# Eight layer steps on one core: VectorE takes q and k ahead of its norm steps in attention 0, the first stacks are loaded by head halves, the last layer's roots move from GpSimd to ScalarE, and two blocks end without GpSimd's drain

## The chip, the cores and the metric

One Trainium2 chip, one core of it. The metric is the device time of one launch in microseconds. The kernel before took 2697.12 us, the median of three runs (2694.36, 2697.12 and 2703.2).

## The reference, cut to what matters

Four layers, each an attention step and a feed-forward step, on 16 batches of 256 tokens by 128 channels (4096 tokens). Every attention has 16 heads. Each of the eight steps is x = _layernorm(x + step(x)), with this normalisation of each token:

```python
def _layernorm(x, axis=-1, eps=1e-05):
    m = jnp.mean(x, axis=axis, keepdims=True)
    v = jnp.var(x, axis=axis, keepdims=True)
    return (x - m) / jnp.sqrt(v + eps)
```

Attention 0 has heads of 64 channels, so that its q, k and v have 1024 columns; attentions 1 to 3 have heads of 8. Attention 1 takes the softmax of negated distances, attention 3 is causal:

```python
# attention 0
Q = (x @ Wq.T + bq).reshape(B, N, H, HD)
K = (x @ Wk.T + bk).reshape(B, N, H, HD)
V = (x @ Wv.T + bv).reshape(B, N, H, HD)
scores = jnp.einsum('bnhd,bmhd->bhnm', Q, K)
w = jax.nn.softmax(scores * (SCALE * adaptive_scale)[None, :, None, None] / TEMP, axis=-1)
attn = jnp.einsum('bhnm,bmhd->bnhd', w, V).reshape(B, N, H * HD)
y = x + (attn @ Wo.T + bo)
mu, var = jnp.mean(y, axis=-1, keepdims=True), jnp.var(y, axis=-1, keepdims=True)
return (y - mu) / jnp.sqrt(var + EPS) * gamma + beta      # then x = _layernorm(x + this)
```

So attention 0 has two normalisations, an inner one with gamma and beta and the outer one of the step. Feed-forward 3, the last step, sends each token to two of eight experts with limited places, adds both weighted results to those of a shared expert, and ends with a normalisation, which is the program's output. The inverse roots of that last normalisation are the ones that the change moves.

## The kernel before

Each of the eight steps is one block of the program: attn0 (`attention_wide`), ffn0 (`routed_layer`), attn1 (`attention_dist`), ffn1, attn2 (`attention_small`), ffn2 (`sign_mlp`), attn3 (`attention_small`, causal) and ffn3 (`routed_layer` with two places for each token, `cap2`). The tokens stand in SBUF as `x_state`, 32 tiles of 128 tokens by 128 channels. The five engines run from one order each, written out by hand by loops over slots, and meet by semaphores. A block ends with each engine's drain and a barrier, then its semaphores are cleared on GpSimd and there is a second barrier (L2785 and L2786).

**Attention 0** (L51 to L484). A unit is two heads of one batch; a batch has U = 8 units, and a slot is one unit. Z_AT, A_AT + 1 and W_AT say in which slot of a batch the steps of the two normalisations run on VectorE: `inner_norm` (L437), `outer_stats` (L419 and L422) and `write_x` (L448). They are even slots. VectorE also takes the maxima of the scores (`row_max`, L399), adds the bias to q and k of the unit two slots ahead (`take_qk`, L410, which empties the PSUM bank `A_M`), turns sums around (`invert`, L404), and in odd slots copies a transposed tile (`take_turned`, L415). `A_M` is one bank shared by the projections of q and k (L255), of v (L263), the transposes of x (L245) and the output projection (L307); before each of them TensorE waits in `bank_free` until the last user's result has been taken. The affine part of the norm, `A_s` (L205 and L208), is GpSimd's; so are the normalised probabilities (L185). ScalarE has the exponentials (L355), the copies of v (`A_V`, L348) and others.

**Attentions 1 to 3.** The projected q and k of a batch are cut into three bf16 parts, stored to DRAM (L621; L1217 in attention 1) and read back stacked on partitions: `stack(b)` on SP's queue issues three loads of `A_QS` and three of `A_KS`, each 24 rows of 16 heads x 256 columns. TensorE's `score(n)` waits for all six of its batch at the first head. In attention 1 the first head also waits for the squared lengths (`n2_in`), whose DMAs stand behind the stack on the same queue.

**Feed-forward 3, its end.** GpSimd fetches with indirect DMAs (`fetch`, L1892) each token tile's result from the second of its experts, 32 fetches in eight groups of four. For each group g VectorE does `add_first` (L2449 and L2453), `add_second` (L2460), `norm_stats` (L2467, L2470 and L2472, which gives `L_veps`) and `write` (L2477, `L_shift`). The root of each group is one GpSimd instruction, `tensor_tensor` with `pow` and an exponent of -0.5 (L1919), put between the fetches of later groups. ScalarE writes the normalised tiles (L2190), after it has copied eight groups of transposed coefficients from PSUM (`L_coefT`, L2186); those come from TensorE's `turn_coef(g)` (L2048), which alternates with the products with them (L2059). A product waits until VectorE has taken the result two groups before. SP stores `out` in eight pieces (L1873).

## Time and profile before

| | |
|---|---|
| profiled execution | 2692.44 us, span 2690.7 us, mean granted clock 0.911 of full speed |
| median of three runs | 2697.12 us |
| busy share of the span | PE 84%, PEld 60%, DVE 59%, ACT 58%, POOL 51% |
| attn0, 0 to 684 us; the rest of the slices below is ffn0 to ffn3 | PE 95.7 to 97.1% busy in each of five stretches of 100 us between 100 and 600 us |
| last block, ffn3 | 2407.7 to 2690.7 us |

The page shows the span in 40 slices of 67 us, each digit the busy share in tenths:

```profile
PE   5999999998294899998399958999799699976783
DVE  3566666666412899998623327667454466643465
ACT  3666666665152899998145524667544277651352
POOL 2454554555235888863133155654321488735346
PEclk9999999999596799999599969999899799987995
```

The time of an execution is the span and a little around it (1.7 us in this one). Small groups of waits matter here, not the shares: the program is a row of eight stages with different limits.

### The profile page before, as it was taken

The numbers are of one execution on the slowest core, as the hardware profiler recorded it, in microseconds if no ns is written. First come the engines' busy times: TensorE is split into PE (matmuls) and PEld (weight loads), VectorE is DVE, ScalarE is ACT, GpSimd is POOL, SyncE is SP. The second block draws the span as 40 slices with busy tenths as digits, with TensorE's granted clock in tenths as the row PEclk, the third lists the DMA queues.
The fourth block names the chain that finished last, engine by engine and source line by source line (L and its number), as shares of the span: only waits on it lengthen the run. The fifth ranks groups of instructions, "written<-read, shape, count | busy, mean of one in ns | idle before, by whom it ended". The sixth has DMA issues, their size and how long they took to land. (4 is left out here: it accounts for less than half of the span.)

```text
span 2690.7 us, 52551 instructions
## 1 busy us (share of the span) xinstructions
PE 2248.2 (84%) x17832; PEld 1619.0 (60%) x17832; DVE 1593.5 (59%) x4357; ACT 1572.2 (58%) x3828; POOL 1361.9 (51%) x2164
## 2 busy tenths in 40 slices
PE   5999999998294899998399958999799699976783
PEld 3667667666193566665289934555345477754682
DVE  3566666666412899998623327667454466643465
ACT  3666666665152899998145524667544277651352
POOL 2454554555235888863133155654321488735346
PEclk9999999999596799999599969999899799987995
DMA  4000000000312322210311134332000333311232
GB/s 164 1 1 1 2 1 1 1 1 1 119 56 69 99 63 80 71 59 1 134 44 47 38 82 115 92 100 80 2 1 1 87 108 100 98 40 52 74 120 74
DMA packets 106506, 153.46 MB, mean 57 GB/s; under 512 B 17330, under 2 KB 78660, under 8 KB 99204
## 3 DMA queue, kind: packets, MB, share of 16 engines
q1 hardware_dynamic: 93956, 127.24, 15.3%
q0 software_dynamic: 12288, 22.86, 3.4%
q8 instruction: 148, 2.42, 0.4%
q14 instruction: 114, 0.93, 0.1%
HBM read 100.87 MB, written 47.19 MB: 55 GB/s over the span
## 5 line engine op out<-in xcount | busy, mean ns | idle before, releaser
L185 POOL TENSOR_SCALAR A_prob<-A_prob,A_rinv 128x256 f32<-128x256 f32 x512 | 254.3, 514 | 325.4 <-DVE A_rinv L404 325.4
L1011 DVE TENSOR_REDUCE A_nmax<-A_S 128x2 f32<-128x512 f32 (+1 forms) x512 | 311.5, 621 | 173.6 <-PE A_S L788 83.5
L940 ACT ACTIVATE A_PT<-A_E 128x512 f32<-128x512 f32 (+1 forms) x512 | 273.0, 551 | 142.3 <-PE A_E L811 65.8
L355 ACT ACTIVATE A_prob<-A_S,A_nmax 128x256 f32<-128x256 f32 x512 | 236.7, 488 | 102.9 <-DVE A_nmax L399 102.9
L1885 POOL DMA_INDIRECT L_xe<-rows,L_index x112 | 106.5, 950 | 231.3 <-PE L_k L1976 112.2
L1608 DVE TENSOR_SCALAR_CACHE_REDUCE A_D<-A_S 128x256 f32<-128x256 f32 x512 | 193.5, 417 | 14.8 <-PE A_S L1391 14.4
L1614 DVE COPY A_PT<-A_T 128x512 f32<-128x512 f32 x256 | 175.3, 687 | 19.4 <-PE A_T L1404 19.3
L1404 PE MATMUL A_T<-ident_sb,A_D 128*128 128x128 f32 x1024 | 160.5, 280 | 27.9 <-ACT A_D L1533 15.1
L2031 PE MATMUL L_k<-L_w,L_hT 128*128 (+1 forms) x1216 | 171.3, 279 | 12.3 <-ACT L_hT L2177 10.7
L2031 PEld LDWEIGHTS L_k<-L_w,L_hT 128*128 128x128 f32 x1216 | 153.8, 195 | 15.9 <-ACT L_hT L2177 12.6
L399 DVE TENSOR_REDUCE A_nmax<-A_S 128x2 f32<-128x512 f32 x256 | 158.7, 681 | 4.7 <-PE A_S L272 4.7
L255 PE MATMUL A_M<-A_xT,A_wqk 128*128 128x256 f32 x512 | 139.0, 394 | 14.8 <-ACT A_xT L341 12.3
L1404 PEld LDWEIGHTS A_T<-ident_sb,A_D 128*128 128x128 f32 x1024 | 116.7, 143 | 57.6 <-ACT A_D L1533 22.6
L1268 POOL TENSOR_TENSOR A_D<-A_D 128x1024 f32<-128x1024 f32 x64 | 120.6, 1891 | 47.1 <-ACT A_D L1528 47.0
L2017 PE MATMUL L_k<-L_xT,L_wr 128*128 128x128 f32 x896 | 131.2, 283 | 13.5 <-issue 9.7
L826 PE MATMUL A_O<-A_PT,A_v 128*32 128x256 f32 (+1 forms) x2048 | 140.2, 368 | 1.4 <-ACT A_OS L946 0.9
L285 PEld LDWEIGHTS A_T<-ident_sb,A_prob 128*128 128x128 f32 x1024 | 116.8, 141 | 40.1 <-issue 31.0
L2429 DVE TENSOR_TENSOR L_hT<-L_silus,L_k 128x512 f32<-128x512 f32 x72 | 49.5, 688 | 146.0 <-PE L_k L2021 76.5
L285 PE MATMUL A_T<-ident_sb,A_prob 128*128 128x128 f32 x1024 | 133.9, 274 | 0.3 <-ACT A_PT L361 0.3
L272 PE MATMUL A_S<-A_QK 64*128 64x256 f32 x1024 | 129.6, 393 | 0.0
L1528 ACT ACTIVATE A_D<-A_D 128x1028 f32<-128x1028 f32 x128 | 127.9, 1051 | 0.2
L299 PE MATMUL A_O<-A_PT,A_V 128*64 128x256 f32 x1024 | 124.9, 385 | 1.5 <-ACT A_OT L368 1.1
(426 smaller groups left out, 6036.9 us busy)
## 6 DMA issues: line engine op xcount, KB each, us to landing
A_QS<-stack_q SPq DMA_DIRECT2D x144, 192.0 KB
A_KS<-stack_k SPq DMA_DIRECT2D x144, 192.0 KB
results<-L_ye SPq DMA_DIRECT2D x48, 256.0 KB
stack_q<-A_parts SPq DMA_DIRECT2D x48, 192.0 KB
stack_k<-A_parts SPq DMA_DIRECT2D x48, 192.0 KB
L_w<-f_w SPq DMA_DIRECT2D x24, 256.0 KB, 6.9
sent<-A_zeros SPq DMA_DIRECT2D x10, 512.0 KB
L_xe<-sent SPq DMA_DIRECT2D x20, 256.0 KB
```

Source lines behind the costliest of these rows:

```text
L185: nc.gpsimd.tensor_scalar(prob[:, n % NP, j, t, :], prob[:, n % NP, j, t, :], rinv[:, n % NP, j, t:t + 1], 1.0, ALU.mult, ALU.mult).then_i ...
L255: i = nc.tensor.matmul(psM[:, j, :], wqk[:, j, g, :], xT[:, b % 2, :], start=True, stop=True)
L285: i = nc.tensor.transpose(psT[j][:, m, t * P:(t + 1) * P], prob[:, n % NP, j, t, m * P:(m + 1) * P], consts["ident"][:])
L355: nc.scalar.activation(prob[:, n % NP, j, t, :], psS[n % 2][j][:, t, :], ACT.Exp, bias=nmax[:, n % NP, j, t:t + 1], scale=1.0, accum_out=r ...
L399: nc.vector.tensor_reduce(nmax[:, n % NP, j, :], psS[n % 2][j][:], AX.X, ALU.max, negate=True).then_inc(maxed, 1)
L826: i = nc.tensor.matmul(psO[32 * j:32 * (j + 1), 0, n0:], v1[:, b % NV, m, h, :], p, start=(m == 0), stop=(m == TB - 1), skip_group_check=True)
L940: nc.scalar.activation(PT[:, n % RING, :], psE[n % 2][:, 0:BLOCKS, :].rearrange("p a b -> p (a b)"), ACT.Exp, scale=scale).then_inc(expd, 1)
L1011: nc.vector.tensor_reduce(nmax[:, b % 2, :, h], view, AX.X, ALU.max, negate=True).then_inc(maxed, 1)
L1404: i = nc.tensor.transpose(T[:, m, t * P:(t + 1) * P], D[:, u % RD, c:c + P], consts["ident"][:])
L1608: nc.vector.tensor_scalar(D[:, u % RD, c:c + SEQ], psS[n % 2][:, t, :], 1e-12, None, ALU.max, ALU.min, accum_out=D[:, u % RD, W + TB * j + ...
L1614: nc.vector.tensor_copy(PT[:, n % RP], psT[n % 2][:]).then_inc(turned_v, 1)
L2031: m = nc.tensor.matmul(psY[q % 2][:, k * P:(k + 1) * P], hT[:, i % HT, f, :], moving, start=(f == 0), stop=(f == NF - 1))
```

## The change

1. In attention 0's order for VectorE, `take_turned`, `take_qk` and `invert` now come ahead of `write_x`, `inner_norm` and `outer_stats` of the same slot.
2. `stack(0)` of attentions 1, 2 and 3 issues twelve loads in place of six, first those of heads 0 to 7, which count on a new semaphore `halved`, then those of heads 8 to 15. `score(0)` waits for `halved`, `score(8)` for the rest. In attention 1 `score(0)` still waits for the lengths.
3. In feed-forward 3 GpSimd issues the 32 fetches in a row. ScalarE loads the function table with the square root ahead of the coefficient copies, takes the root of each group (`L_deviation`), and writes the group before it; VectorE takes the reciprocal of that root and refines it in three more operations before the shift, each waiting for the one ahead of it.
4. The blocks of attention 2 and of feed-forward 3 end without GpSimd's drain, and after them there is neither a clearing of semaphores nor a second barrier (attention 2's are cleared after ffn2).

```diff
@@ attention_wide, VectorE @@
                     if (n := y_half(slot)) is not None:
                         take_y(n)
+                    if (n := pair(slot, LAG_T)) is not None and by_vector(n):
+                        take_turned(n)
+                    if (n := pair(slot, -QK_AHEAD)) is not None:
+                        take_qk(n)
+                    if slot % 2 == 1 and (n := pair(slot)) is not None:
+                        invert(n)
                     if (b := at(slot, W_AT)) is not None:
                         write_x(b)
                     if (b := at(slot, Z_AT)) is not None:
                         inner_norm(b)
                     if (b := at(slot, A_AT + 1)) is not None:
                         outer_stats(b)
-                    if (n := pair(slot, LAG_T)) is not None and by_vector(n):
-                        take_turned(n)
-                    if (n := pair(slot, -QK_AHEAD)) is not None:
-                        take_qk(n)
-                    if slot % 2 == 1 and (n := pair(slot)) is not None:
-                        invert(n)
@@ attention_small, and likewise attention_dist: SyncE and TensorE @@
-        with nc.Block() as block:
+        with nc.Block(no_gpsimd_drain=not causal) as block:
...
+                    if b == 2:
+                        sp.wait_ge(halved, 96)
...
-                    for a in range(PARTS):
-                        rows = slice(a * PARTS * HD, (a + 1) * PARTS * HD)
...
+                    for some, signal in [(slice(0, H * SEQ // 2), halved), (slice(H * SEQ // 2, H * SEQ), stacked[i])] if b == 0 else [(slice(0, H * SEQ), stacked[i])]:
+                        size = some.stop - some.start
+                        for a in range(PARTS):
+                            rows = slice(a * PARTS * HD, (a + 1) * PARTS * HD)
+                            sp.dma_start(QS[rows, buf, :, :].rearrange("r h n -> r (h n)")[:, some],
+                                         scratch["q"][i].rearrange("a (c h) n -> (a c) (h n)", h=H)[:, some]).then_inc(signal, 16)
...
-                    if h == 0:
+                    if n == 0:
+                        pe.wait_ge(halved, 96)
+                    if n == H // 2 or h == 0 and b:
                         pe.wait_ge(stacked[b % 2], 96 * (b // 2 + 1))
@@ routed_layer @@
-        with nc.Block() as block:
+        with nc.Block(no_gpsimd_drain=cap2) as block:
...
-                for g in range(NG):
-                    for t in range(g * G, (g + 1) * G):
-                        fetch(1, t)
-                    if g >= 2:
-                        root(g - 2)
-                root(NG - 2)
-                root(NG - 1)
+                for t in range(NT):
+                    fetch(1, t)
...
                 if cap2:
+                    nc.scalar.preload_act_table_set("sqrt_and_others")
...
+                def root(g):
+                    s = slice(g * G, (g + 1) * G)
+                    act.wait_ge(var_ready, g + 1)
+                    nc.scalar.activation(deviation[:, s], veps[:, s], ACT.Sqrt).then_inc(rooted, 1)
...
+                if cap2:
+                    for g in range(NG):
+                        root(g)
+                        if g:
+                            write_out(g - 1)
+                    write_out(NG - 1)
...
                     dve.wait_ge(rooted, g + 1)
+                    nc.vector.reciprocal(rstd[:, s], deviation[:, s]).then_inc(refined, 1)
+                    dve.wait_ge(refined, 3 * g + 1)
+                    nc.vector.scalar_tensor_tensor(out=deviation[:, s], in0=rstd[:, s], scalar=-0.5, in1=veps[:, s], op0=ALU.mult, op1=ALU.mult).then_inc(refined, 1)
+                    dve.wait_ge(refined, 3 * g + 2)
+                    nc.vector.tensor_tensor(deviation[:, s], deviation[:, s], rstd[:, s], ALU.mult).then_inc(refined, 1)
+                    dve.wait_ge(refined, 3 * g + 3)
+                    nc.vector.scalar_tensor_tensor(out=rstd[:, s], in0=deviation[:, s], scalar=1.5, in1=rstd[:, s], op0=ALU.add, op1=ALU.mult).then_inc(shift_ready, 1)
+                    dve.wait_ge(shift_ready, 2 * g + 1)
                     nc.vector.scalar_tensor_tensor(out=shift[:, s], in0=mv[:, s, 0], scalar=-1.0, in1=rstd[:, s], op0=ALU.mult, op1=ALU.mult).then_inc(shift_ready, 1)
@@ the loop over steps @@
-            nc.clear_and_free_semaphores([s for s in free if s not in left])
-            nc.all_engine_barrier()
+            used += [s for s in free if s not in left]
+            if step not in ("attn2", "ffn3"):
+                nc.clear_and_free_semaphores(used)
+                used = []
+                nc.all_engine_barrier()
```

The order of VectorE's instructions in attention 0, in the slot of a batch that has `outer_stats` (`A_s` is the affine result that GpSimd makes, `A_M` the shared PSUM bank, `A_rsum` the sums of the exponentials). Before:

```order
L404 RECIPROCAL A_rinv<-A_rsum 128x4
L399 TENSOR_REDUCE A_nmax<-A_S 128x2 x4
L419 BN_STATS A_stats<-A_s 128x6 x2
L422 BN_AGGR A_mv<-A_stats 128x2 x2
L410 TENSOR_TENSOR A_QK<-A_M,A_bqk 128x512
L462 TENSOR_REDUCE logit<-A_gated 128x4
L404 RECIPROCAL A_rinv<-A_rsum 128x4
```

and with the change:

```order
L404 RECIPROCAL A_rinv<-A_rsum 128x4
L399 TENSOR_REDUCE A_nmax<-A_S 128x2 x4
L410 TENSOR_TENSOR A_QK<-A_M,A_bqk 128x512
L419 BN_STATS A_stats<-A_s 128x6 x2
L422 BN_AGGR A_mv<-A_stats 128x2 x2
L462 TENSOR_REDUCE logit<-A_gated 128x4
L404 RECIPROCAL A_rinv<-A_rsum 128x4
```

Only L410 has moved, from behind the statistics to ahead of them; L437 and L448 are passed in the same way in the two other slots.

The end of GpSimd's order in feed-forward 3 (`L_rows` are the fetched results, `sent` the scattered tokens, `L_veps` the variances). Of the 44 fetches in the first row of them, 32 are the first experts' and 12 those of groups 0 to 2 of the second. Before:

```order
L1889 DMA sent<-x_state,row 10240x128 x64
L1892 DMA L_rows<-results,row 128x128 x44
L1919 TENSOR_TENSOR L_rstd<-L_veps,L_mhalf 128x4
L1892 DMA L_rows<-results,row 128x128 x4
L1919 TENSOR_TENSOR L_rstd<-L_veps,L_mhalf 128x4
L1892 DMA L_rows<-results,row 128x128 x4
```

(four more such pairs follow, and three roots at the end), and with the change:

```order
L1889 DMA sent<-x_state,row 10240x128 x64
L1902 DMA L_rows<-results,row 128x128 x64
L1844 UNCONDITIONAL_BRANCH
```

The eight roots have gone, and the fetches stand in a row. The end of ScalarE's order in the same place, as a difference (`L_coefT` are the transposed coefficients, `L_k` the PSUM bank, `L_acc` the sums that are normalised):

```order
 L2177 ACTIVATE L_hT<-L_k,L_b1t 128x128 x12
-L2186 ACTIVATE L_coefT<-L_k 9x512 x8
-L2190 ACTIVATE x_state<-L_acc,L_shift,L_rstd 128x128 x32
-L1831 UNCONDITIONAL_BRANCH
+L2184 ACT_TABLE_LOAD
+L2187 ACTIVATE L_coefT<-L_k 9x512 x8
+L2192 ACTIVATE L_deviation<-L_veps 128x4 x2
+L2197 ACTIVATE x_state<-L_acc,L_shift,L_rstd 128x128 x4
+L2192 ACTIVATE L_deviation<-L_veps 128x4
+L2197 ACTIVATE x_state<-L_acc,L_shift,L_rstd 128x128 x4
```

The first two roots now stand behind all eight coefficient copies, and every later root ahead of one group's writes.

## Rows read from the trace of the kernel before

**Rows 1.** Waits, 60 to 660 us: engine line <- releaser: total us, times, longest
```profile
DVE A_stats L419 <- POOL A_s L208: 31.0, 14, 2.2
PE A_M L263 <- DVE A_QK L410: 20.1, 14, 1.7
```

**Rows 2.** Timeline, attn0, VectorE: start, busy us, instruction [idle before <- releaser]
```profile
316.83 0.49 DVE L419 BATCH_NORM_STATS2 A_stats<-A_s 128x6 f32<-128x128 f32 x2 [2.23 <-POOL A_s L208]
317.45 0.67 DVE L410 TENSOR_TENSOR A_QK<-A_M,A_bqk 128x512 f32<-128x512 f32 x1
```

**Rows 3.** Timeline, the same batch, TensorE and ScalarE
```profile
318.17 1.13 PE L263 MATMUL A_M<-A_wv,A_xT 128*128 128x512 f32 x2 [1.45 <-DVE A_QK L410]
320.01 1.11 PE L255 MATMUL A_M<-A_xT,A_wqk 128*128 128x256 f32 x4
...
317.88 0.27 ACT L355 ACTIVATION_READ_ACCUMULATOR A_prob<-A_S,A_nmax 128x1 f32 x1
```

**Rows 4.** Timeline, attn3, SP's DMA issues
```profile
2105.64 0.33 SPq L627 DMA_DIRECT2D A_QS<-stack_q  x1
...
2120.64 0.32 SPq L627 DMA_DIRECT2D A_QS<-stack_q  x1
```

**Rows 5.** Timeline, attn3, TensorE's first scores of batches 0 and 1
```profile
2119.66 0.29 PE L785 MATMUL A_S<-A_KS,A_QS 72*128 72x128 bf16 x1 [8.97 <-DMA A_KS<-stack_k]
...
2134.18 0.28 PE L785 MATMUL A_S<-A_KS,A_QS 72*128 72x128 bf16 x1 [2.08 <-DMA A_KS<-stack_k]
```

**Rows 6.** GpSimd's drains at the ends of blocks: durations ns min/median/max, first and last start
```profile
L606 POOLq DRAIN  x2: 1667/4282/6898, 1932.8 to 2403.9; - x2
L1831 POOLq DRAIN  x3: 8964/9167/12080, 782.1 to 2680.6; - x3
```

**Rows 7.** Timeline, the last of attn2 and the first of ffn2
```profile
1934.81 0.38 ACT L971 ACTIVATE XT<-A_X 128x256 f32<-128x256 f32 x1 [0.78 <-PE A_X L868]
1940.76 0.61 POOL L2597 CAST L2m_xp<-XT 128x512 bf16<-128x512 f32 x1 [7.65 <-SPq L2591]
```

**Rows 8.** Timeline, ffn3, GpSimd between fetches
```profile
2644.53 0.94 POOL L1892 DMA_INDIRECT L_rows<-results,row  x1 [0.30 <-issue]
2645.49 1.06 POOL L1919 TENSOR_TENSOR L_rstd<-L_veps,L_mhalf 128x4 f32<-128x4 f32 x1
2646.73 1.01 POOL L1892 DMA_INDIRECT L_rows<-results,row  x1 [0.18 <-issue]
```

**Rows 9.** Timeline, ffn3, VectorE: shifts and the last variance
```profile
2667.09 0.15 DVE L2477 SCALAR_TENSOR_TENSOR L_shift<-L_mv,L_rstd 128x4 f32<-128x4 f32 x1
...
2671.48 0.16 DVE L2477 SCALAR_TENSOR_TENSOR L_shift<-L_mv,L_rstd 128x4 f32<-128x4 f32 x1
...
2680.35 0.17 DVE L2472 TENSOR_SCALAR L_veps<-L_mv 128x4 f32<-128x4 f32 x1
```

**Rows 10.** Timeline, ffn3, TensorE's last coefficient transposes, ScalarE's last copy and writes
```profile
2647.26 1.02 PE L2048 MATMUL L_k<-ident_sb,L_coef 128*9 128x128 f32 x4
...
2655.59 0.59 ACT L2186 ACTIVATE L_coefT<-L_k 9x512 f32<-9x512 f32 x1 [10.77 <-remote]
...
2680.62 3.19 ACT L2190 ACTIVATE x_state<-L_acc,L_shift,L_rstd 128x128 f32<-128x128 f32 x8 [1.25 <-DVE L_shift L2477]
```

**Rows 11.** Waits, 2640 to 2692 us, VectorE for its own results
```profile
DVE L_veps L2472 <- remote: 3.7, 2, 1.9
...
DVE L_mv L2470 <- DVE L_stats L2467: 1.6, 3, 0.8
```

**Rows 12.** Chain of waits: start, us, what (2430 to 2500 us, then the last block's end)
```profile
2459.95 34.40 another core or an unknown queue
...
2675.48 2.49 DMA L_rows<-results,row
```

**Rows 13.** Timeline, ffn3, GpSimd's last scatter of the burst
```profile
2487.77 0.95 POOL L1889 DMA_INDIRECT sent<-x_state,row  x1 [0.30 <-issue]
```

**Rows 14.** ffn3, all second-half fetches: ns min/median/max
```profile
L1892 POOL DMA_INDIRECT L_rows<-results,row x64: 938/947/1337, 2579.0 to 2675.5; - x64
```

More of the change, by code:

```diff
@@ L624, in stack @@
                     after(sp, turned, H * (b - NBUF + 1))
-                    for a in range(PARTS):
-                        rows = slice(a * PARTS * HD, (a + 1) * PARTS * HD)
-                        sp.dma_start(QS[rows, buf, :, :].rearrange("r h n -> r (h n)"),
-                                     scratch["q"][i].rearrange("a (c h) n -> (a c) (h n)", h=H)).then_inc(stacked[i], 16)
-                        sp.dma_start(KS[rows, buf, :, :].rearrange("r h n -> r (h n)"),
-                                     scratch["k"][i, a].rearrange("(c h) n -> c (h n)", h=H).unsqueeze(0).to_broadcast([PARTS, HD, H * SEQ])).then_inc(stacked[i], 16)
+                    for some, signal in [(slice(0, H * SEQ // 2), halved), (slice(H * SEQ // 2, H * SEQ), stacked[i])] if b == 0 else [(slice(0, H * SEQ), stacked[i])]:
[4 more added lines that the diff above has]
+                                         scratch["q"][i].rearrange("a (c h) n -> (a c) (h n)", h=H)[:, some]).then_inc(signal, 16)
+                            sp.dma_start(KS[rows, buf, :, :].rearrange("r h n -> r (h n)")[:, some],
+                                         scratch["k"][i, a].rearrange("(c h) n -> c (h n)", h=H)[:, some].unsqueeze(0).to_broadcast([PARTS, HD, size])).then_inc(signal, 16)
                 for s in range(FIRST, LAST + 4):
@@ L1215, in stack @@
                     after(sp, stacked[i], 96 * (b // 2))
+                    if b == 2:
+                        sp.wait_ge(halved, 96)
                     for j, n in enumerate("qk"):
@@ L1219, in stack @@
                     after(sp, scored, H * (b - NBUF + 1))
-                    for a in range(PARTS):
-                        rows = slice(a * PARTS * HD, (a + 1) * PARTS * HD)
-                        sp.dma_start(QS[rows, buf, :, :].rearrange("r h n -> r (h n)"),
-                                     scratch["q"][i].rearrange("a (c h) n -> (a c) (h n)", h=H)).then_inc(stacked[i], 16)
-                        sp.dma_start(KS[rows, buf, :, :].rearrange("r h n -> r (h n)"),
-                                     scratch["k"][i, a].rearrange("(c h) n -> c (h n)", h=H).unsqueeze(0).to_broadcast([PARTS, HD, H * SEQ])).then_inc(stacked[i], 16)
+                    for some, signal in [(slice(0, H * SEQ // 2), halved), (slice(H * SEQ // 2, H * SEQ), stacked[i])] if b == 0 else [(slice(0, H * SEQ), stacked[i])]:
+                        size = some.stop - some.start
+                        for a in range(PARTS):
+                            rows = slice(a * PARTS * HD, (a + 1) * PARTS * HD)
+                            sp.dma_start(QS[rows, buf, :, :].rearrange("r h n -> r (h n)")[:, some],
+                                         scratch["q"][i].rearrange("a (c h) n -> (a c) (h n)", h=H)[:, some]).then_inc(signal, 16)
+                            sp.dma_start(KS[rows, buf, :, :].rearrange("r h n -> r (h n)")[:, some],
+                                         scratch["k"][i, a].rearrange("(c h) n -> c (h n)", h=H)[:, some].unsqueeze(0).to_broadcast([PARTS, HD, size])).then_inc(signal, 16)
                 def lengths(b):
@@ L1384, in score @@
                     q, k, S = QS[0:KR, b % NBUF, h, :], KS[0:KR, b % NBUF, h, :], psS[n % 2]
+                    if n == 0:
+                        pe.wait_ge(halved, 96)
+                    if n == H // 2 or h == 0 and b:
+                        pe.wait_ge(stacked[b % 2], 96 * (b // 2 + 1))
                     if h == 0:
-                        pe.wait_ge(stacked[b % 2], 96 * (b // 2 + 1))
                         pe.wait_ge(n2_in, 32 * (b + 1))
@@ L1803, in routed_layer @@
         fetched = [[sem(f"fetched{k}{g}") for g in range(NG)] for k in range(K)] if cap2 else None
-        stated, aggregated, var_ready, rooted, shift_ready = (
-            sem("stated"), sem("aggregated"), sem("var_ready"), sem("rooted"), sem("shift_ready"))
+        refined, stated, aggregated, var_ready, rooted, shift_ready = (
+            sem("refined"), sem("stated"), sem("aggregated"), sem("var_ready"), sem("rooted"), sem("shift_ready"))
         if cap2:
@@ L2186, in _, with write_out @@
                         nc.scalar.activation(coefT[:, 4 * g:4 * g + 4, :].rearrange("e t p -> e (t p)"), psC[g % 2][0:E + 1, :], ACT.Copy).then_inc(coefT_out, 1)
-                for g in range(NG if cap2 else 0):
-                    act.wait_ge(shift_ready, g + 1)
+                def root(g):
+                    s = slice(g * G, (g + 1) * G)
+                    act.wait_ge(var_ready, g + 1)
+                    nc.scalar.activation(deviation[:, s], veps[:, s], ACT.Sqrt).then_inc(rooted, 1)
+                def write_out(g):
+                    act.wait_ge(shift_ready, 2 * g + 2)
                     for t in range(g * G, (g + 1) * G):
                         nc.scalar.activation(x_state[:, t, :], y[:, t, :], ACT.Identity, bias=shift[:, t:t + 1], scale=rstd[:, t:t + 1]).then_inc(written, 1)
+                if cap2:
[4 more added lines that the diff above has]
+                    write_out(NG - 1)
             @block.vector
```

14 lines of the change are left out of this document (4 added, 10 removed).

## The prediction

> **What bounds the kernel now.** I read first the busy shares in 40 slices, to see which stage has which limit, then for each place that the change touches the waits of its window and the timeline of the engines that meet there, and last the chain of waits at the end. In attention 0 TensorE is over 95% busy, so the few waits it has are the time that can be won. [rows 1] shows the one wait in its steady stretch that is not of its sequencer: 14 times, once for each batch that is under way, the projection of v (L263) waits for VectorE's L410, which has to empty `A_M`; together 20.1 us. [rows 2, 3] show why. L410 starts at 317.45, behind the statistics (L419), which waited 2.23 us for GpSimd's affine result. VectorE's time is not short there, its order is. At the starts of attentions 1 to 3 TensorE waits for the stacked loads [rows 5]. At the end of attn2 GpSimd's drain takes 6.9 us [rows 6], and 5.6 us lie between the last work's end at 1935.2 and the next block's first at 1940.8 [rows 7]. In ffn3 the end follows the fetches, then VectorE's steps, then ScalarE's eight last tiles [rows 8 to 10].
>
> **Attention 0.** L410 needs only the bank's result, which TensorE had given before the wait began: L410 can run where VectorE waits for L419, from 316.83 - 2.23 = 314.60 us. It takes 0.67 us and fits into the 2.23, so the statistics are not late by it. TensorE then goes on 1.4 us sooner. What is late next is ScalarE: its exponentials of the slot end at 318.15 [rows 3], and only then can it copy v (0.6 us, to 318.75), for which TensorE's next user of the bank (L255, at 320.01 - 1.45 = 318.56) waits. That leaves at most 0.2 us of wait. In the two other slots L410 passes L437 and L448, which gives TensorE nothing, as it does not wait there. 14 x 1.44 = 20.1, of which I take **-20 us**; bounds -17 (0.2 us back each time) and -20.5. Moving `take_turned` and `invert` costs nothing: they are in odd slots, the norm steps in even ones.
>
> **Head halves.** In attn3 stack(0) is issued from 2105.64 and the loads of batch 1 from 2120.64 [rows 4]; scores begin at 2119.66 and those of batch 1 at 2134.18, both after a wait for their loads [rows 5]. Half the bytes should be in after half of the 14 us from issue to score, so score(0) comes some 6.5 us earlier. But score(16) needs batch 1's loads, which are behind the same bytes of batch 0 in the same queues. The scores of batch 0 were through before the wait of 2.08 us at 2134.18, so that starting them sooner lengthens that wait and no more. Six more issues of 0.3 to 0.7 us on SP put batch 1's stores about 3 us later, but these then wait behind the loads anyway. **0 us** in each of three places; bounds from +2 us (the queue is late by the issues) to -6.5 us in attn2 and attn3. In attn1 score(0) still waits for the lengths, whose two DMAs now stand behind twelve loads: nothing can be won there.
>
> **Attn2's drain.** All other engines are done at 1935.2; the drain of GpSimd, the barrier, the clearing and the second barrier end at 1940.7. One barrier is left, some 0.3 us. **-5.2 us**, bounds -4.5 and -5.5. The drain's work may still have to be done, but GpSimd has time at the end of ffn2 before its next full drain.
>
> **The end of ffn3.** What is removed: five roots between fetches. With a root the distance from one fetch to the next is 2.20 us, without one 1.25 (0.94 and 0.30) [rows 8]: 5 x 0.95 = 4.8 us, so the last fetch is issued at about 2670.7 and not 2675.5, and GpSimd's drain (9.0 us from 2680.6, which sets the end at 2690.7 [rows 6]) goes. What is added: on VectorE four more small steps for each group, each dependent on the one before it, 0.17 us busy [rows 9] and 0.02 to wait for itself, 0.76 us. A group took 2671.48 - 2667.09 = 4.39 us of VectorE and will take 5.16, about the pace of four fetches (5.0). And a **new wait**: VectorE's first `write` needs ScalarE's first root, and that now stands behind all eight coefficient copies. The last of them ran only at 2655.59, after 10.77 us of waiting, though TensorE's transposes had by the profile ended at 2648.3 [rows 10]. Behind that `write` VectorE holds add_second, the statistics, and every later group.
>
> From the first `write` to the last variance VectorE has 4 groups of 5.16 and 2 shorter ones (no add_first left) of 3.27: 27.2 us. Then `write` of group 6 (0.84), and ScalarE's last eight tiles, 3.19 [rows 10], with the signal 4.15 in all. The store's landing and the barrier take 2.8 us after that (before: the last tile ended at 2683.8, its store landed 2.5 us later by the fetch's 2.49 in [rows 12], and 0.3 for the barrier). With the first `write` at W the end is at W + 34.2.
> - Last copy at 2655.6 as before: its 0.59, the root and two signals give W = 2656.6, the end 2690.8: +0.1.
> - Besides, VectorE waited for its own results in this stretch, 3.7 + 1.6 = 5.3 us [rows 11], while GpSimd issued fetches back to back. Those fetches still run until 2670.7, over the first three groups: +5.3.
>
> **+5.4 us**, bounds -7 (below) and +32 (below). The step with the most weight is when that signal comes, and here the trace shows a behaviour without its cause: signals are late during long bursts of indirect DMAs. In the scatters' burst ScalarE got none for 34.40 us, to 2494.35 [rows 12], 5.6 us past the end of the last scatter, 2488.7 [rows 13]. With the roots gone from between the fetches nothing interrupts this burst; I take the moment of the same signal in the same place, since it is the nearest row. ScalarE's table load costs nothing: it stands ahead of the copies, in which ScalarE waits 10.77 us anyway.
>
> **A rule against it.** The longest of 64 such fetches took 1.34 us and the median 0.95 [rows 14], beside VectorE's work. The Trainium skill, page "SBUF — State Buffer", section "SBUF: two separate sides" (the box on "DVE blocks DMA"), states that GpSimd can't write the descriptors of its DMAs while VectorE runs certain operations from SBUF to SBUF; by that, 32 added operations slow the fetches. The rows speak against it, and it is the fourth rival below.
>
> **Sum:** -20 - 5.2 + 0 + 5.4 = -19.8 us on the profiled execution's 2692.4, which stands 4.7 us under the median of three. On the median: 2697.1 - 19.8 = **2677 us**.
>
> **Rivals.**
> 1. *The last coefficient signal is on time.* TensorE ends at 2648.3, W = 2649.4, the end 2683.6: -7 in place of +5.4, total -32, **2665 us**. For it: by the profile TensorE had ended, and nothing else is shown that ScalarE could wait for. Against: the 10.77 us, and a burst without pauses can hardly be kinder than one with them. Chance 0.17.
> 2. *Signals are held until the burst is over.* After the fetches' end at 2670.7, plus 5.6 us as after the scatters, at 2676.3: W = 2677.3, the end 2711.5, +21; total -4, **2693 us**. Chance 0.09.
> 3. *Slower than before.* The same hold lasts as long as ScalarE's in the scatters, 34.40 us [rows 12], from 2648.3 to 2682.7: W = 2683.7, end 2717.9, and VectorE's own 5.3 on it, +32.5; total +7.3, **2704 us**. It decides from a signal later than 2675.4 us (W = 2676.4, where W + 34.2 + 5.3 = 2690.7 + 25.2). Against: it would outlast the burst by 12 us. With a smaller gain in attention 0 it passes +8. Chance 0.05.
> 4. *Fetches slow down beside VectorE.* All 32 at the longest 1.34 for 0.95: +12.5 us, the last lands at 2685.7, the last variance is there 2.5 us later, the end 4.15 + 2.8 after that, at 2695.1: +4.4, hidden in the forecast's +5.4, but with rival 1 the total would be -21, **2676 us**. Chance 0.03.
> 5. *Halves pay.* -6.5 in attn2 and in attn3, total -33, **2664 us**. For it: a wait of 9 us ends sooner. Against: the loads of batch 1. Chance 0.09.
> 6. *The wait of attention 0 moves,* to ScalarE's copy or GpSimd's probabilities, and half comes back: total -10, **2687 us**. Chance 0.07. That the change doesn't move L410 is excluded, the order shows it moved.
>
> **Numbers.** The forecast has 0.50. The range of 8 in 10 goes from rival 1 with some spread of the runs (they differed by up to 9 us) to rival 2: **2662 to 2692**. A difference under 0.3%, 8 us, can't be told from none. Faster by more: forecast, rivals 1, 4, 5, 6, together 0.86; same: rival 2 and half of 3 with mixtures, 0.10; slower: 0.04.
>
> **What would show it.** In the waits of attention 0 `PE A_M L263 <- DVE A_QK L410` is gone, TensorE at 99%, each batch 1.4 us shorter. attn3's first scores come 6 us sooner, those of batch 1 where they were. Between attn2's last copy and ffn2's first cast lies 0.3 us. In ffn3 the first reciprocal of VectorE stands near 2656.6 less the time won before (25 us); if it stands at 2649 less that, rival 1 holds, if behind the last fetch, rivals 2 or 3. The forecast is wrong if TensorE has a new wait of over 0.5 us a batch in attention 0, or if the last block, 283.0 us before (from 2407.7), is shorter by over 5 us or longer by over 12.

## The result, and the profile after

The changed kernel took 2689.07 us (median of 7 runs, 2682.89 to 2697.44), the kernel before on the same chip 2703.2 (7 runs, 2694.36 to 2707.57, the three of above among them): ratio 0.9955 with a 95% interval of 0.9936 to 0.9974, some 12 us faster, with 7 to 17 in the interval. On another chip it was 0.998 (0.9961 to 1.0). 20 us had been forecast. The profiled execution took 2694.38 us, 2 us more than that of before, so that it has to be read stage by stage (from one barrier to the next; attn2 to ffn2's first instruction):

| stage | before | after | difference |
|---|---|---|---|
| attn0 | 684.6 | 665.9 | -18.7 |
| ffn0, attn1, ffn1 | 136.8, 468.1, 274.4 | 135.6, 469.2, 271.7 | -2.8 |
| attn2 with its drain | 376.9 | 382.2 | +5.3 |
| ffn2 | 147.5 | 146.8 | -0.7 |
| attn3 | 319.5 | 321.7 | +2.2 |
| ffn3 | 282.9 | 299.4 | +16.5 |

**Attention 0.** The page of the changed kernel, and two stretches of its windows (columns: start and end, length, then busy us and instructions of PE, PEld, DVE, ACT, POOL, granted clock, DMA share, GB/s):

```profile
span 2692.7 us, 52583 instructions
...
PE 2258.5 (84%) x17832; PEld 1623.9 (60%) x17832; DVE 1598.9 (59%) x4389; ACT 1575.2 (59%) x3837; POOL 1352.7 (50%) x2155
```

```profile
100.00:200.00 100.00, 99.90 (x691) 70.26 (x687) 64.58 (x143) 68.75 (x231) 55.10 (x108) 1.00 0.01 1
500.00:600.00 100.00, 99.90 (x698) 71.41 (x698) 67.91 (x153) 69.64 (x236) 53.15 (x103) 1.00 0.00 1
```

TensorE went from about 96% to 99.9%. In the waits from 60 to 660 us the row of TensorE for L410 [rows 1] is gone. What is left for VectorE, and the slot of one batch in the timeline:

```profile
DVE A_QK L410 <- PE A_M L255: 55.1, 106, 1.4
...
DVE A_stats L419 <- POOL A_s L208: 17.9, 15, 1.5
```

```profile
308.29 0.69 DVE L410 TENSOR_TENSOR A_QK<-A_M,A_bqk 128x512 f32<-128x512 f32 x1 [0.29 <-PE A_M L255]
310.24 0.49 DVE L419 BATCH_NORM_STATS2 A_stats<-A_s 128x6 f32<-128x128 f32 x2 [1.25 <-POOL A_s L208]
```

L410 now stands inside the wait for `A_s`, which shrank from 2.23 [rows 2] to 1.25 us: with the 0.29 us ahead of L410 and its 0.69 these are the same 2.23.

**Attn2's end.** The last of attn2 and the first of ffn2:

```profile
1924.01 0.38 ACT L977 ACTIVATE XT<-A_X 128x256 f32<-128x256 f32 x1 [0.78 <-PE A_X L874]
1924.74 0.61 POOL L2619 CAST L2m_xp<-XT 128x512 bf16<-128x512 f32 x1 [2.42 <-SPq L2613]
```

0.35 us lie between them where 5.6 did [rows 7]. The drain's work has only moved: GpSimd's drain at the end of ffn2 took 0.04 us before and takes 6.60 us now, from 2024.4 us on, 47 us before that block ends, so that nobody waits for it. 5.2 us are saved, and yet the stage is 5.3 us longer. The windows of the stage's stretch from 30 to 330 us, of before and of after:

```profile
1593.90:1893.90 300.00, 269.46 (x2235) 155.91 (x2235) 205.78 (x450) 185.28 (x438) 167.86 (x299) 0.92 0.33 95
```

```profile
1572.50:1872.50 300.00, 270.91 (x2134) 155.35 (x2135) 198.00 (x430) 178.62 (x421) 165.19 (x292) 0.87 0.33 95
```

TensorE is as busy, but at a granted clock of 0.87 in place of 0.92 it does 101 of 2235 matmuls fewer. The records of the clock put most of it in one place: 93 us into the stage (about 1635 to 1666 us) TensorE stood at 1.2 GHz, the lower of its two levels, for 30.7 us, where the kernel before had only a short dip. That much more time at half the clock costs at most 15 us, an estimate from these figures, and enough for the 10.5 us that are to be explained (5.2 + 5.3).

**Attn3.** The first scores of batches 0 and 1:

```profile
2098.57 0.29 PE L791 MATMUL A_S<-A_KS,A_QS 72*128 72x128 bf16 x1 [4.84 <-DMA A_KS<-stack_k]
...
2117.93 0.29 PE L791 MATMUL A_S<-A_KS,A_QS 72*128 72x128 bf16 x1 [6.89 <-DMA A_KS<-stack_k]
```

Counted from the block's start (2071.5, before 2088.3), the first scores come at 27.1 us and not 31.4 [rows 5], 4.3 sooner. Batch 1's come at 46.4 and not 45.9, and the wait before them grew from 2.08 to 6.89 us: the gain of batch 0 is given back there in full.

**Ffn3.** Timelines of GpSimd, ScalarE and VectorE around the end of the fetches. "remote" stands where the profile finds nothing on this core that ended the wait, "issue" where it shows nothing that was waited for:

```profile
2655.52 0.94 POOL L1902 DMA_INDIRECT L_rows<-results,row  x1 [0.30 <-issue]
```

```profile
2630.79 0.59 ACT L2187 ACTIVATE L_coefT<-L_k 9x512 f32<-9x512 f32 x1 [7.56 <-PE L_k L2048]
2657.41 0.59 ACT L2187 ACTIVATE L_coefT<-L_k 9x512 f32<-9x512 f32 x1 [26.04 <-remote]
2657.90 0.28 ACT L2192 ACTIVATE L_deviation<-L_veps 128x4 f32<-128x4 f32 x2
```

```profile
2658.12 0.18 DVE L2491 RECIPROCAL L_rstd<-L_deviation 128x4 f32<-128x4 f32 x1 [25.71 <-issue]
...
2663.53 0.17 DVE L2491 RECIPROCAL L_rstd<-L_deviation 128x4 f32<-128x4 f32 x1
...
2668.69 0.17 DVE L2491 RECIPROCAL L_rstd<-L_deviation 128x4 f32<-128x4 f32 x1
```

GpSimd's last fetch instruction ended at 2656.46. Only 0.95 us later did ScalarE's last coefficient copy run, after ScalarE had stood idle for 26.04 us; TensorE's transposes had, by the profile, ended at 2634.3. VectorE, which needs ScalarE's root, stood for 25.71 us. After that it went on with one wait of 0.27 us, 5.16 us for a group. Not every signal in the burst was held: the first six of the eight copies ran within 0.05 us of TensorE's transposes, the last of them 6 us after the first fetch began; the seventh was 1.4 us late, the eighth 23.1.

### The profile page after: what moved, and what is told of

Read it like the earlier page. It is cut to its first block and busy times, and to the rows that moved or that the text cites. A ratio compares the mean times of both kernels' runs of the same rounds, so it can differ in the third digit from the quotient of the medians.

```text
span 2692.7 us, 52583 instructions
## 1 busy us (share of the span) xinstructions
PE 2258.5 (84%) x17832; PEld 1623.9 (60%) x17832; DVE 1598.9 (59%) x4389; ACT 1575.2 (59%) x3837; POOL 1352.7 (50%) x2155
## 5 line engine op out<-in xcount | busy, mean ns | idle before, releaser
L1417 PE MATMUL A_T<-ident_sb,A_D 128*128 128x128 f32 x1024 | 161.3, 281 | 27.1 <-ACT A_D L1546 14.5
L410 DVE TENSOR_TENSOR A_QK<-A_M,A_bqk 128x512 f32<-128x512 f32 x128 | 88.5, 691 | 73.1 <-PE A_M L255 72.1
```

What stands on the lines that cost most here:

```text
L1417: i = nc.tensor.transpose(T[:, m, t * P:(t + 1) * P], D[:, u % RD, c:c + P], consts["ident"][:])
```

## The experiments

All ratios are to the kernel before on the same chip. The two numbers of the last block by which they are told apart: its length, and when ScalarE's last coefficient copy ran, counted from the start of the first of the 32 fetches (24.8 us before, 40.8 after). TensorE's transposes for it end there at 17.5 to 17.7 us. Lengths of blocks are those of one profiled execution each. Experiments 1 to 4 ran on one chip, 5 to 8 on a second, 9 to 12 on a third, 13 to 15 on a fourth, 16 and 17 on a fifth and a sixth.

**1. Without part 3 (no_tail).** The changed kernel with the `routed_layer` of before, its drain, clearing and barrier.

> The changed kernel with the last block as it was before (roots on GpSimd between the fetches, its drain, clearing and barrier). Theory A (the change to the last block costs 16.5 us, because ScalarE's last coefficient copy is held until the fetches end): the last block takes 283 us again, and the whole is about 16 us under the changed kernel, some 24 to 28 us under the kernel before (about 0.99 of it). Theory B (the last block's time is another execution's accident): the last block takes anything, and the ratio to the kernel before stays near 0.9955.

Ratio 0.9902 (0.9879 to 0.9925), the last block 285.2 us. Theory A holds: the rest of the change is worth 27 us. The copy ran at 24.3 us again.

**2. Part 3 alone (tail_alone).**

> The kernel before with the last block of the changed one, and nothing else of the change. Theory A: the last block takes 299 us in place of 283, the whole is 14 to 18 us slower than before (ratio 1.006). Theory B: within 5 us of before. The stages ahead of the last block are as before; their differences between two executions show how far the clock alone moves them.

Ratio 1.0067 (1.0046 to 1.0087), 18 us slower; the block took 306.5 us, 21 more than in no_tail on the same chip, and the copy ran at 45.2. The two experiments split the change: -27 and +18 us.

**3. Tiny pauses (fetch_pauses).**

```diff
                 for t in range(NT):
                     fetch(1, t)
+                    if t % 4 == 3:
+                        nc.gpsimd.memset(pause[:, t:t + 1], 0.0)
```

> The changed kernel with one tiny GpSimd memset after every fourth of the 32 fetches. Theory A1 (signals are held by the unbroken row of indirect DMAs, and any other instruction of GpSimd lets them through): the last coefficient copy runs soon after TensorE's transposes, within 10 us and not 24, VectorE's first reciprocal comes 10 us or more sooner, and the last block falls from 299 to about 285 us. Theory A2 (it is the length of the pause that counts, 1 us of a root, or the hold has nothing to do with the fetches): the copy stays at the end of the fetches, the last block at 299 to 301 us.

Ratio 0.9956 (0.9934 to 0.9977), the block 306.3 us, the copy at 45.3, behind the last fetch at 38.8:

```profile
2668.50 0.59 ACT L2189 ACTIVATE L_coefT<-L_k 9x512 f32<-9x512 f32 x1 [16.29 <-remote]
```

A1 falls as it was put: the block is as long as without the memsets (306.5 us in tail_alone, on the same chip). Two things limit the reading. The memsets took 0.11 us each and fitted into the 0.30 us between two fetches, the last of which began at 38.8 us as before, so that no pause arose. And the copy ahead of the last, held for 20.5 us, ran at 28.4, in the midst of the burst: what is held is not always held to its end.

**4. Tiny pauses in the scatters (scatter_pauses).** The same after every fourth of the 64 scatters, on no_tail.

> The kernel of no_tail with a tiny GpSimd memset after every fourth scatter of the last block. If a memset lets signals through (A1), ScalarE's wait of 34 us in the scatters (L_sT) falls below 10 us, and the last block is shorter by up to 20 us, as far as the scatters' own end does not set what follows. If not (A2), nothing changes by over 2 us.

Ratio 0.9892 (0.9872 to 0.9912) beside no_tail's 0.9902, the block 286.8 beside 285.2 us, ScalarE's longest wait in the scatters 31.2 us beside 34.6. No effect on the block. The copy ran only at 35.9 us in this trace, although the five roots stood between the fetches; more on that under experiment 8.

**5. The roots ahead of the last copy (roots_first).**

```diff
                 if cap2:
+                    for g in range(NG - 1):
+                        copy_coef(g)
                     for g in range(NG):
                         root(g)
                         if g:
                             write_out(g - 1)
+                        if g == 1:
+                            copy_coef(NG - 1)
                     write_out(NG - 1)
```

> The changed kernel with ScalarE's last coefficient copy moved behind its first two roots and the first group's writes, so that VectorE's first write no longer waits for that copy. Theory A (only TensorE's signal to ScalarE is held): VectorE's first reciprocal comes about 16 us after the first fetch (42 in the changed kernel), the next stop is add_first(5), which needs a product of TensorE; the last block takes 277 to 285 us, 15 to 22 less than the changed kernel's 299. Rival A3 (all signals between engines are held in the fetches' burst, those of VectorE and ScalarE too, or the hold hits the next product): the first reciprocal is early, but VectorE then stands until the fetches end all the same, and the block keeps over 293 us.

Ratio 0.9965 (0.9952 to 0.9979), the block 302.4 us. VectorE's timeline in the fetches' burst:

```profile
2640.84 0.18 DVE L2496 RECIPROCAL L_rstd<-L_deviation 128x4 f32<-128x4 f32 x1 [2.33 <-ACT L_deviation L2193]
...
2644.36 0.16 DVE L2500 TENSOR_TENSOR L_deviation<-L_deviation,L_rstd 128x4 f32<-128x4 f32 x1 [1.24 <-DVE L_deviation L2498]
2645.76 0.16 DVE L2502 SCALAR_TENSOR_TENSOR L_rstd<-L_deviation,L_rstd 128x4 f32<-128x4 f32 x1 [1.24 <-DVE L_deviation L2500]
...
2654.88 0.87 DVE L2486 BATCH_NORM_STATS2 L_stats<-L_acc 128x6 f32<-128x128 f32 x4 [6.47 <-remote]
...
2663.98 0.17 DVE L2491 TENSOR_SCALAR L_veps<-L_mv 128x4 f32<-128x4 f32 x1 [4.71 <-remote]
```

The first write came early, 21.4 us after the first fetch, and nothing was won: A3 holds. From some 14 us into the burst on, most waits of VectorE cost 1.2 to 6.5 us, those for its own last result too, which take 0.02 to 0.04 us behind the burst. From the first reciprocal to the shift VectorE took 6.3 us there (2640.84 to 2647.18), and 0.8 behind the burst. Many of these waits are 1.24 us, the distance between the starts of two fetches (0.94 and 0.30).

**6. Head halves alone (halves_alone).**

> The kernel before with only the first stacks cut into head halves. Forecast theory: within 2 us of before; the first scores of attn2 and attn3 come some 6 us sooner, those of batch 1 1 us later. Rival C (TensorE, started early and then idle again until batch 1, has its clock lowered at another time, which costs 5 us or more in attn2): 3 to 10 us slower than before. Rival D (halves pay): 5 us or more faster.

Ratio 1.000 (0.9981 to 1.002). The forecast of nothing holds, within some 5 us either way.

**7. Roots left on GpSimd, both drains gone (roots_kept).**

```diff
-        with nc.Block() as block:
+        with nc.Block(no_gpsimd_drain=cap2) as block:
...
-            if step != "attn2":
+            if step not in ("attn2", "ffn3"):
```

(to no_tail)

> The changed kernel with the roots of the last block on GpSimd between the fetches as before, but without the drain, the clearing and the barrier behind that block. The last store lands 4.5 us before the end of the kernel before, so that the last block should take 278.5 to 280 us, 4 less than with the drain, and the whole be 4 us under the 0.9902 of the kernel that keeps them (0.9887). If the unfinished drain is paid at the program's end anyway, it stays at 0.990.

Ratio 0.9873 (0.9851 to 0.9895); the block 281.8 us, its end 55.9 us after the first fetch and not 59.9. The drain behind the last block is worth its 4 us, and no later wait takes them back.

**8. The same with whole stacks (whole_stacks).**

> The kernel of roots_kept with the stacks loaded whole again: attention 0's order and the missing drains are all that is left of the change. Forecast theory: equal to roots_kept within 2 us. Rival C: 3 to 10 us faster than roots_kept. Rival D: 5 us or more slower.

Ratio 0.9894 (0.9873 to 0.9914). The 5.8 us between the medians of 7 and 8 lie within the intervals. In the profiled executions attn2 took 372.1 us in roots_kept and 383.5 in whole_stacks, and the windows of the two (30 to 330 us of the stage) say why:

```profile
1581.90:1881.90 300.00, 267.07 (x2230) 155.32 (x2231) 206.17 (x447) 185.04 (x436) 168.49 (x299) 0.92 0.33 96
```

```profile
1581.30:1881.30 300.00, 271.23 (x2123) 154.77 (x2124) 197.26 (x429) 177.62 (x420) 164.97 (x290) 0.87 0.33 95
```

Here it is the kernel without halves that has the lower clock. Neither rival C nor D is borne out: the 371 to 385 us of attn2 go with the clock of the execution and not with the halves. whole_stacks has the same 30.7 us at 1.2 GHz, 93 us into the stage, as the changed kernel; roots_kept has only a short dip there, as the kernel before.

In whole_stacks the last copy ran at 34.3 us, and not at 24 to 26 as in the kernel before, no_tail, halves_alone and roots_kept. The two copies ahead of it had been held too, so that it came later in the row, and TensorE's transposes for it ended only at 22.2 us; scatter_pauses (35.9 us) shows the same. In all these traces each held copy ran 1.2 to 4.7 us after the start of one of GpSimd's roots.

**9. Pauses of a root's length (long_pauses).** The changed kernel, in which GpSimd computes an unused power of 128x4 elements at the five places where roots had stood.

```diff
                 for t in range(NT):
                     fetch(1, t)
+                    if t % G == G - 1 and 2 * G < t < NT - 1:
+                        nc.gpsimd.tensor_tensor(spare[:, t - 3:t + 1], mhalf[:, t - 3:t + 1], mhalf[:, t - 3:t + 1], ALU.pow)
```

> The changed kernel with a GpSimd power of 128x4 elements (1 us, its result unused) at the five places between the fetches where the roots stood before. Theory E (a pause of 1 us after four fetches lets signals through, one of a tiny memset does not): the last coefficient copy runs some 25 us after the first fetch, as in the kernel before, and not 41 to 45, the last block takes 285 to 290 us and not 299 to 306. Rival F (the roots' place has nothing to do with it; it is the new waits between engines that are slow): the copy comes at 40 or later, and the fetches' end, 5 us later than in the changed kernel, puts the block's end over 300.

This chip is another sort: the kernel before took 2587.72 us on it and not 2700, and no such hold shows there: ffn0 takes 121 us in place of 137, ffn1 260 in place of 272 to 280, the last block 231.3. The copy ran at 17.6 us, with the transposes. Ratio 0.9885 (0.9863 to 0.9906). For theory E that says nothing.

**10. The attention 0 part alone (attn0_alone), on that chip.**

> The kernel before with attention 0's order of the changed kernel and nothing else: attn0 ends at 666 us and not 685, the whole is 18 to 20 us faster (ratio 0.993). If the time won there were given back by the following stages (the clock), the ratio would be over 0.996.

Ratio 0.9919 (0.99 to 0.9938), 21 us (17 to 26); attn0 666.4 us. Nothing was given back.

**11. Pauses in the scatters (scatter_long).** roots_kept with such a power after every fourth scatter.

> The kernel of roots_kept with such a 1 us power after every fourth of the 64 scatters of the last block. Theory E: ScalarE's wait of 34 us in the scatters becomes a row of short ones, and the last block gets shorter, by up to 15 us, as far as the 8 us that the pauses add before the experts' rows are complete do not take it back. Rival: the 8 to 16 us of pauses are all that changes, the block is 5 to 15 us longer.

Ratio 0.9951 (0.9934 to 0.9968), the block 246.3 us beside the 229.7 of the next experiment: where nothing is held, the pauses lose 16.6 us.

**12. Its base (roots_kept_2).**

> The kernel of roots_kept again, as the base of scatter_long on its chip: the last block 280 to 283 us, the ratio to the kernel before 0.986 to 0.990. attn2's time, which was between 371 and 385 us in ten executions with and without head halves, shows once more whether it goes with the halves or with the execution.

Ratio 0.9874 (0.9854 to 0.9894), the block 229.7 us, attn2 343.0. In the waits of its last block the rows "<- remote" of ScalarE are missing:

```profile
ACT L_sT L2154 <- PE L_k L1975: 32.2, 32, 5.5
...
ACT L_coefT L2199 <- PE L_k L2061: 19.1, 7, 6.7
```

**13. The changed kernel again (after_2).**

> The changed kernel again, as the base of the other two on their chip. If the chip holds signals (ffn0 over 130 us, the last block 299 to 306): last copy 41 to 45 us after the first fetch, ratio to before about 0.9955. If it does not (ffn0 121 us): copy at 17.6, the first write at 19, the last block 9 us shorter than before in place of 16 longer, ratio about 0.987, as rival 1 of the prediction had it.

A chip that holds signals (ffn0 135.8): copy at 39.4, just as the last fetch ran (39.1 to 40.0), the block 299.4 us as in the first trace, ratio 0.998 (0.9961 to 1.0) and not the 0.9955 of the first chip.

**14. Long pauses beside it (long_pauses_2).**

> The changed kernel with five GpSimd powers of 1 us between the fetches. On a chip that holds signals, theory E: the copy at 25 to 30 us after the first fetch, the last block 8 to 15 us shorter than after_2's. Rival F: the copy no earlier than in after_2, the block 2 to 5 us longer. On a chip that holds none: 5 to 6 us longer than after_2, since the fetches end 5 us later.

Copy at 21.3, the block 281.0 us, ratio 0.9912 (0.9896 to 0.9929): 18 us shorter than after_2's on the same chip, by five powers that nobody uses; 8 to 15 had been expected. ScalarE's and GpSimd's timelines:

```profile
2638.29 0.59 ACT L2192 ACTIVATE L_coefT<-L_k 9x512 f32<-9x512 f32 x1 [7.27 <-remote]
```

```profile
2637.07 0.95 POOL L1905 DMA_INDIRECT L_rows<-results,row  x1 [0.30 <-issue]
2638.05 1.04 POOL L1932 TENSOR_TENSOR L_spare<-L_mhalf 128x4 f32<-128x4 f32 x1
2639.28 1.01 POOL L1905 DMA_INDIRECT L_rows<-results,row  x1 [0.19 <-issue]
```

The copy starts within the second pause. Theory E holds, rival F falls.

**15. An unbroken burst without the new steps (roots_after).** roots_kept with all eight roots behind the 32 fetches and VectorE's writes last.

> The kernel of roots_kept with the 32 fetches in a row and all eight roots of GpSimd behind them, VectorE's writes last. On a chip that holds signals, theory E: the copy 40 us or more after the first fetch though nothing new stands on ScalarE and VectorE. Rival F: the copy at 24 to 36 us, as in the kernels with roots between the fetches.

Copy at 42.9, the block 300.3 us, ratio 0.9978 (0.9961 to 0.9996). The burst alone holds the copy.

**16. Pauses in the scatters again (scatter_long_2, with roots_kept_3).**

> On a chip that holds signals, theory E: ScalarE's longest wait in the scatters falls from 33 us to under 10 us, and the last block is between 10 us shorter and 5 longer than that of roots_kept_3, since the pauses cost 16 us by themselves (measured on the chip that holds none) and the hold some 50 (283 against 230 us, in all its bursts together). If pauses do nothing there: the wait stays over 30 us and the block is 16 us longer. On a chip that holds none: 16 us longer again.

> The base of scatter_long_2: last block 280 to 283 us on a chip that holds signals, 230 on one that does not; ratio to before 0.987 on either.

A chip that holds nothing once more (before 2588.87 us): ratios 0.9939 (0.9923 to 0.9956) and 0.9889 (0.9872 to 0.9905), blocks 246.6 and 230.0 us.

**17. And once more (scatter_long_3).**

> On a chip that holds signals (ffn0 over 130 us): theory E: ScalarE's longest wait in the scatters under 10 us, the last block 270 to 286 us beside the 281.8 of roots_kept there, ratio to before 0.983 to 0.989. If pauses do nothing there: a wait over 30 us and a block of about 298 us, ratio 0.993. On a chip that holds none (ffn0 121 us): 246 us and 0.994 to 0.995 as measured.

A chip that holds signals (before 2710.88 us): ratio **0.982** (0.9795 to 0.9845), 49 us faster than before, the block 264.8 us beside roots_kept's 281.8. The waits in the last block of roots_kept, and then of this kernel:

```profile
ACT L_sT L2154 <- remote: 44.9, 4, 33.2
```

```profile
ACT L_sT L2161 <- PE L_k L1982: 32.5, 29, 5.5
```

The hold of 33 us is gone, at the price of the 16.6 us that the pauses cost where nothing is held. roots_kept was measured on another chip of this sort (0.9873, 0.9851 to 0.9895), so that the 17 us between the blocks compare two chips; the intervals of the two ratios lie apart. scatter_long beats the kernel before on both sorts of chip, and on this sort its ratio is the lowest of all; where nothing is held roots_kept is better. The changed kernel was at 0.9955 and 0.998 on chips that hold.

## Why the prediction was wrong, step by step

- **Attention 0, -20 us: right.** -18.7 us in the trace, -21 by the ratio of experiment 10. The wait left for ScalarE's copy did not show: TensorE is at 99.9%. L410 took the place that it was given in L419's wait.
- **Head halves, 0: right,** and by the mechanism named: the wait of batch 1 grew by 4.8 us where 4.3 were won. The first scores came 4.3 us sooner, 6.5 had been estimated. Rival 5 (halves pay 13 us) falls with experiment 6.
- **Attn2's drain, -5.2: right,** 0.35 us in place of 5.6. GpSimd's work was done at the end of ffn2 in its spare time, as the prediction had it. The saving does not show in the profiled stage, because that execution had a lower clock there; the 10.5 us that are lacking are put down to it. after_2, the same kernel, took 371.1 us at 0.93, and whole_stacks and roots_kept show both clocks without any link to the change. I had not priced that, although the runs shown differed by 9 us.
- **Ffn3, +5.4: wrong, this is the step that failed.** It measured +16.5 (299.4 us, and 299.4 again in after_2). What is arithmetic in it was right: the first write at W gives an end at W + 34.2 = 2692.3, measured 2692.7; a group took 5.16 us; and the last fetch came 5.8 us sooner after the first, where 4.8 were forecast. (Five roots stood between the fetches, as the prediction counts them: in the order of before three more pairs follow the two shown, not four.) What failed is the term "last copy at 2655.6 as before", +0.1 us, and the sentence that it rests on, that I take the moment of the same signal in the same place, since it is the nearest row. Counted from the first fetch the signal came 16.0 us later, at 40.8 and not 24.8. That row was measured with roots between the fetches, and the change takes them out; the prediction used just that argument against rival 1 (a burst without pauses can hardly be kinder), and not against its own term.
- **What happened there.** Experiments 14 and 15 show that these roots were what let the signal through: with five pauses of 1 us it comes at 21 us, in an unbroken burst at 39 to 45, with or without the new steps. (With the roots in place it came at 24 to 26 us in five traces and at 34 to 36 in two.) So it is rival 2 that happened, in its mechanism; it was priced at +21, and +16.5 came, since the hold ended 0.95 us behind the last fetch and not 5.6. By the prediction's own signs the forecast fell: the last block is longer by over 12 us, and the first reciprocal stands behind the last fetch.
- **The sum.** The measured parts give -18.7 - 5.2 + 16.5 = -7.4 us, which is within the 7 to 17 us of the first chip, at the edge, and within the 0 to 11 of after_2's; what lies between -7.4 and the 12 us of the first chip is not explained beyond the spread of the clock. That the measured 2689.07 us lies in the range forecast is owed to rival 2, which sets the range's upper end, and not to the forecast's reason. It is luck too that the end of the fetches that rival 2 goes by, 2670.7, fits the measured one (39.9 us after the first fetch in both): there the start of the last fetch is taken for its end, and the roots' removal is priced 1 us too low.
- The other term of ffn3, 5.3 us for VectorE's own late signals, measured nothing: by the time VectorE wrote, the burst was over, and behind it its waits for itself are 0.02 to 0.04 us and one of 0.27.
- **The rule against it** (the Trainium skill, page "SBUF — State Buffer", section "SBUF: two separate sides"), rival 4: the page ties this to VectorE's 2-port modes and names an fp32 copy from SBUF to SBUF. Whether any of the added operations (a reciprocal and three with two inputs for each group) runs in such a mode no row shows, so that "32 added operations slow the fetches" went further than the page. In the changed kernel they ran behind the burst and could not test it. In long_pauses six groups of them ran beside the fetches, whose median was 0.955 us, the longest 1.09, with 0.30 between them where no pause stood. The trace shows nothing of it for these operations.
- Rival 1 (all signals on time) needs a chip that holds none; the changed kernel was not run on one. long_pauses there had the copy at 17.6 us, the moment of rival 1. Rivals 3 (a hold of 34 us) and 6 (the wait of attention 0 moves) did not happen.

## What to carry to other kernels

An instruction that looks like lost time between two DMAs may be what lets the others' signals pass. So before a pause in a row of GpSimd's indirect DMAs is taken out, look at what the other engines wait for meanwhile ("remote" waits that end with or just behind the burst). And don't take the moment of a signal from a trace in which the pause still stands. On a chip that holds signals, chains of small dependent steps belong behind such a burst, not beside it: 0.8 us and 6.3 in experiment 5. And where a bank or buffer is emptied by an engine that waits for something else just ahead of it in its order, moving that one instruction ahead can be worth the whole wait: 18.7 us of 20.1 here.

## What the runs showed that I had not expected

- On one sort of chip signals between the other engines, and an engine's waits for its own results, are delayed while GpSimd issues a row of indirect DMAs, 1.25 us apart without a pause: by 0.3 us up to 34.5 (ScalarE in the scatters). In the fetches it began some 13 us into the row; what was due up to 9 us into it came on time. A power of 1 us after every fourth DMA lets them through or shortens the delay, a memset of 0.11 us, which fits between two DMAs, does not. Why, no run shows, nor whether it is the time between two DMAs that counts or the instruction that fills it: a bare delay was not tried.
- Two of the chips do not do this. There the kernel before takes 2588 us and not 2700. Of roots_kept, which has traces on both sorts, ffn0 is 15 to 16 us shorter there, ffn1 19, attn2 29 to 30 and ffn3 52. Attn2 runs there at a granted clock of 0.96 to 0.97 over its middle 300 us, and not 0.92. What makes these chips different is open; nothing in the kernel does.
- On the chips that hold signals attn2 took 371 to 385 us, in executions of kernels that differ there in the halves and the drain at most, with a granted clock of 0.87 to 0.93 over its middle 300 us. That is a larger spread than any other stage shows that the experiments left alone (ffn1: 272 to 280). Why the stretch of 30.7 us at 1.2 GHz comes in some executions only is open.
- GpSimd's drain behind the last block is pure time. Without it roots_kept ended 4.0 us earlier after the first fetch than the kernel before (55.9 and 59.9 us).
